# Tiles at multiples of 512 bytes, the last expert batch by token chunk, TensorE's attention groups without a loop, and two output additions in other places

## The reference, cut to what matters

```
x:[64,64,512]
cond[b] = weights[subj[b]]^T x[b] + bias                  # 64x64 per batch element
h   = cond @ WA + bA ; kv, q = halves of h                # each 128 wide
kR  = rope(h @ WB + bB) ; qR = rope(h @ WC + bC)          # 64 wide, q for 16 heads
attn: scores = (q WUQ)(kv WUK)^T + qR kR^T, causal softmax, times (kv WUV), then @ WZ + bZ
x   = x + attn
flat = x @ W^T + adapter(x)                               # low rank, by batch element
logits = flat @ Wg + bg ; top 2 of 4 experts ; each expert takes its top 1024 tokens
y_e = gelu(flat[tokens] @ W1[e]) @ W2[e] * p ;  x[tokens] += y_e
```

## Time and profile before

| | |
|---|---|
| time, median of 3 runs | 1913.26 us (1910.33 to 1914.07) |
| the profiled execution | 1914.91 us, of which the span from the first to the last instruction is 1912.7 us |
| mean granted TensorE clock | 0.985 of full speed |
| busy time | PE 1820.7 us, DVE 925.2 us, ACT 630.4 us, POOL 703.3 us |
| absorb weights | 0 to 47 us of the span |
| attention | 47 to 950 us, 111.3 us for a group |
| routing | 950 to 1163 us |
| experts | 1163 to 1893.3 us, about 90.5 us for a batch |
| after the last matmul | 1893.3 to 1912.7 us |

### The profile page before, as it was taken

One profiled execution on the slowest core, in us unless ns is written; L12 is line 12 of the kernel. 1 busy time (PEld: TensorE's weight loads), 2 busy tenths in 40 slices (PEclk: granted clock), 3 DMA queues, 4 the chain that ended last, 5 costly groups with the idle time before them and its releaser, 6 DMA issues. The chain is left out here.

```text
span 1912.7 us, 29404 instructions
## 1 busy us (share of the span) xinstructions
PE 1820.7 (95%) x10664; PEld 1417.9 (74%) x10664; DVE 925.2 (48%) x1581; ACT 630.4 (33%) x1088; POOL 703.3 (37%) x525
## 2 busy tenths in 40 slices
PE   6799999999999999999999997999999999999996
PEld 4577776767777676777687776888888888888884
DVE  4565667566666656656423783242423333333321
ACT  4333333333333333333223112333333333333331
POOL 1231322123132212313000034565657575757563
PEclk9999999999999999999999998999999999999998
DMA  7000101010010201002132115033304220522001
GB/s 261 23 1 17 52 6 62 7 61 2 17 51 6 62 7 62 1 17 62 37 106 105 61 61 191 19 88 110 66 0 110 99 55 0 132 88 44 9 13 22
DMA packets 68587, 104.80 MB, mean 55 GB/s; under 512 B 12304, under 2 KB 29456, under 8 KB 68496
## 3 DMA queue, kind: packets, MB, share of 16 engines
q1 hardware_dynamic: 53568, 76.92, 12.1%
q0 software_dynamic: 7200, 16.78, 4.8%
q10 hardware_dynamic: 7728, 9.71, 1.4%
HBM read 78.23 MB, written 25.17 MB: 54 GB/s over the span
## 5 line engine op out<-in xcount | busy, mean ns | idle before, releaser
L1858 DVE CAST hh<-hid 128x512 fp32r<-128x512 f32 x128 | 92.5, 723 | 453.1 <-ACT hid L1803 453.1
L1728 POOL TENSOR_TENSOR w1l<-w_raw,w1h 128x512 fp32r<-128x512 f32 x112 | 185.1, 1653 | 153.3 <-ACT w1h L1795 153.2
L441 POOL TENSOR_TENSOR prob<-prob,rinv 128x512 f32<-128x512 f32 x64 | 70.4, 1100 | 465.4 <-DVE rinv L700 465.4
L95 PE MATMUL bank_o<-Mh,mix_h 128*128 128x512 f32 x512 | 211.4, 413 | 20.5 <-DVE x_res L707 19.1
L95 PE MATMUL e_h<-xh,w1h 128*128 (+1 forms) x512 | 203.5, 397 | 5.6 <-POOL w1l L1728 5.6
L96 PE MATMUL e_h<-xl,w1h 128*128 (+1 forms) x512 | 202.6, 396 | 0.0
L97 PE MATMUL e_h<-xh,w1l 128*128 (+1 forms) x512 | 202.5, 395 | 0.0
L97 PE MATMUL bank_o<-Mh,mix_l 128*128 128x512 f32 x512 | 202.1, 395 | 0.0
L96 PE MATMUL bank_o<-Ml,mix_h 128*128 128x512 f32 x512 | 201.7, 394 | 0.0
L95 PE MATMUL e_y<-w2h,hh 128*128 128x512 f32 x512 | 201.2, 393 | 0.0
L96 PE MATMUL e_y<-w2l,hh 128*128 128x512 f32 x512 | 200.6, 392 | 0.0
(11 more groups left out here) (303 smaller groups left out, 3486.9 us busy)
## 6 DMA issues: line engine op xcount, KB each, us to landing
w_raw<-in_W_dram SPq DMA_DIRECT2D x56, 512.0 KB, 4.5
stage<-in_x_dram SPq DMA_DIRECT2D x8, 1024.0 KB, 5.8
x_res<-in_x_dram SPq DMA_DIRECT2D x32, 256.0 KB, 3.5
out_dram<-x_res SPq DMA_DIRECT2D x32, 256.0 KB, 2.0
flat_dram<-flat_sb ACTq DMA_DIRECT2D x32, 256.0 KB, 2.0
rows<-out_dram SPq DMA_DIRECT2D x4, 1024.0 KB, 5.3
stage<-in_W_dram SPq DMA_DIRECT2D x8, 512.0 KB, 5.4
x_res<-out_dram SPq DMA_DIRECT2D x3, 1024.0 KB, 5.1
```

What stands on the lines that cost most here:

```text
L95: nc.tensor.matmul(out, ah, bh, start=start and n == 0, stop=False)
L441: nc.gpsimd.tensor_tensor(prob[:, i % 2, :, :], prob[:, i % 2, :, :], rinv[:, :].unsqueeze(2).to_broadcast([P, HB, C]), ALU.mult).then_inc ...
L1728: nc.gpsimd.tensor_tensor(w1l[:, k, :, :], w1_at(pair, chunk), w1h[:, k, :, :].bitcast(F32), ALU.subtract).then_inc(S["w1_lo"], 1)
L1858: nc.vector.tensor_copy(hh[:, k, :], hid[:, k, :]).then_inc(S["h_hi"], 1)
```

## The change

Allocation: every tile that TensorE reads starts at a multiple of 512 bytes. Small tiles go to the front, to the end of the early region (`SMALL_AT`) or behind the large ones, and `align` fills what is left. Line numbers move by one to some sixty for that. The constant column `part` becomes a table and a transfer of its own.

TensorE's attention program is written out for all 8 groups; the other engines keep the loop. TensorE's program grows from 1881 to 4019 rows.

```diff
@@ absorb_weights, VectorE
-                if i == 1:
+                if i == 2:
                     dve.wait_ge(small_in, SMALL)
...
-                if i in (1, 2):
-                    spread_weights(nc, K, dve, 0, range((i - 1) * GB // 2, i * GB // 2))
+                    spread_weights(nc, K, dve, 0, range(GB))
@@ attention, VectorE
                 queries_rope(g, 6)
+                x2_tile(g, 0)
                 queries_rope(g, 7)
-                x2_tile(g, 0)
...
-                    queries_rope(g + 1, 0)
-                    queries_rope(g + 1, 1)
+                    for u in range(UB - 1):
+                        queries_rope(g + 1, u)
                 x2_tile(g, 5)
                 if more:
-                    queries_rope(g + 1, 2)
-                    queries_rope(g + 1, 3)
+                    queries_rope(g + 1, UB - 1)
@@ attention, TensorE
-            over_groups(pe, first, body)
+            first()
+            for g in range(NG):
+                body(g, g < NG - 1)
@@ experts, GpSimd, last batch
-                    scatter(b, range(CH))
+                    w1_low(END - 2, 0, b, PAIRS - 1, 0)
+                    w2_low(END - 3, 1, b, PAIRS - 2, 1)
+                    w1_low(END - 1, 1, b, PAIRS - 1, 1)
+                    w2_low(END - 2, 2, b, PAIRS - 1, 0)
+                    w2_low(END - 1, 3, b, PAIRS - 1, 1)
+                    pool.wait_ge(S["index_out"], NB)
+                    for c in range(CH):
+                        pool.wait_ge(S["y_ev"], b * CH + c + 1)
+                        pool.indirect_dma_start(out_rows, ..., y_sb[:, c, :], ...)
@@ experts, TensorE, last batch
+            def held(b):
+                hidden(END - 4, 0, b)
+                spend(END - 5, 1)
+                for k in range(1, HELD):
+                    hidden(END - HELD + k, k % 2, b)
+                for c in range(CH):
+                    cols = slice(c * P, (c + 1) * P)
+                    for k in range(HELD):
+                        if c == 0:
+                            pe.wait_ge(S["h_lo"], END - HELD + k + 1)
+                            pe.wait_ge(S["w2_lo"], END - HELD + k + 1)
+                        last = split_product(nc, bank_y[c][:, :], [((hh[:, k, cols], hl[:, k, cols]),
+                                                                    (w2h[:, k, :], w2l[:, k, :]))],
+                                             start=False, stop=k == HELD - 1)
+                    last.then_inc(S["y_mm"], 1)
@@ allocation
+LINE = 512
+def align(nc, ctx, name):
+    short = -(-(-nc.sbuf_base // 32) * 32) % LINE
+    if short:
+        ctx.enter_context(nc.sbuf_tensor(f"pad_{name}", [1, short // 4], F32))
```

More of the change, by code:

```diff
@@ L55 @@
 TABLES = {
-    "always": {"ident": P, "ones": P, "part": 1},
+    "always": {"ident": P, "ones": P},
+    "column": {"part": 1},
     "attend": {"mask": NU // 2 * C, "cosq": NU * C, "sinq": NU * C, "cosk": C, "sink": C},
@@ L1674, in experts @@
         Y0 = 2
+        END = NB * HC
         def over_batches(eng, first, body):
@@ L1693, in rounds @@
             after_two()
-            with eng.Fori(1, LOOP) as i:
+            with eng.Fori(1, LOOP if more else LOOP - 1) as i:
                 two(i)
-            last = b * HC + HC
-            one(last - 2, 0, (b + 1, 0, 0) if more else None, (b, PAIRS - 1, 1))
-            one(last - 1, 1, (b + 1, 0, 1) if more else None, (b + 1, 0, 0) if more else None)
+            if more:
+                last = b * HC + HC
+                one(last - 2, 0, (b + 1, 0, 0), (b, PAIRS - 1, 1))
+                one(last - 1, 1, (b + 1, 0, 1), (b + 1, 0, 0))
         def out_free(eng, b):
@@ L1834, in first @@
                 one(1, 1, (0, 1, 1), (0, 1, 0))
+            def held(b):
+                gelu(END - 4, 0, 0)
+                w1_high(END - 2, 0, b, PAIRS - 1, 0)
+                act.wait_ge(S["y_mm"], END - 4 + Y0)
+                w2_high(END - 3, 1, b, PAIRS - 2, 1)
+                gelu(END - 3, 1, 1)
+                w1_high(END - 1, 1, b, PAIRS - 1, 1)
+                w2_high(END - 2, 2, b, PAIRS - 1, 0)
+                gelu(END - 2, 0, 2)
+                w2_high(END - 1, 3, b, PAIRS - 1, 1)
+                gelu(END - 1, 1, 3)
+                out_free(act, b)
+                for c in range(CH):
+                    act.wait_ge(S["y_mm"], END - HELD + Y0 + c + 1)
+                    nc.scalar.activation(y_sb[:, c, :], bank_y[c][:, :], ACT.Copy,
+                                         scale=R["gate"][:, bass.ds(b * CH + c, 1)]).then_inc(S["y_ev"], 1)
             def body(b, more):
-                for i in range(LOOP):
+                for i in range(LOOP if more else LOOP - 1):
                     for k in range(2):
                         one(b * HC + 2 * i + 2 + k, k, (b, i + 2, k), (b, i + 1 + k, 1 - k))
+                if not more:
+                    held(b)
+                    return
                 last = b * HC + HC
[L1841 to L1849, removed]
+                x_high(b + 1)
+                one(last - 2, 0, (b + 1, 0, 0), (b, PAIRS - 1, 1))
+                one(last - 1, 1, (b + 1, 0, 1), (b + 1, 0, 0))
+                one(last, 0, (b + 1, 1, 0), (b + 1, 0, 1), between=lambda: gated(b))
+                one(last + 1, 1, (b + 1, 1, 1), (b + 1, 1, 0))
             over_batches(act, first, body)
@@ L1885, in body @@
                     index_in(b + 1)
-                with dve.Fori(0, LOOP) as i:
+                with dve.Fori(0, LOOP if more else LOOP - 1) as i:
                     for k in range(2):
@@ L1892, in body @@
                 nc.vector.tensor_copy(tok_out[:, :], R["token"][:, bass.ds(b * CH, CH)]).then_inc(S["index_out"], 1)
-                if more:
-                    x_low(b + 1)
+                if not more:
+                    for k in range(HELD):
+                        one(END - HELD + k, k)
+                    return
+                x_low(b + 1)
                 one(last - 2, 0)
                 one(last - 1, 1)
-                if more:
-                    one(last, 0)
+                one(last, 0)
                 gated(b)
-                if more:
-                    one(last + 1, 1)
+                one(last + 1, 1)
             over_batches(dve, first, body)
@@ L1942, in body @@
                 n = b * HC
-                with pe.Fori(0, LOOP) as i:
+                with pe.Fori(0, LOOP if more else LOOP - 1) as i:
                     for k in range(2):
@@ L1960, in body @@
                 spend(last - 2, 0)
-                if more:
-                    pe.wait_ge(S["xt_lo"], b * TC + TC)
-                    hidden(last, 0, b + 1)
+                pe.wait_ge(S["xt_lo"], b * TC + TC)
+                hidden(last, 0, b + 1)
                 spend(last - 1, 1, stop=True)
[L1965 to L1968, removed]
+                hidden(last + 1, 1, b + 1)
+                pe.wait_ge(S["y_ev"], (b + 1) * CH)
+                spend(last, 0, start=True)
             over_batches(pe, first, body)
@@ L1989, in block_program @@
         K.parts = {}
+        load_table(nc, ctx, K, "column")
+        for name, shape in (("wg", [P, TC, NE]), ("bias", [P, 5])):
+            K[name] = ctx.enter_context(nc.sbuf_tensor(name, shape, F32))
+        K.update(bA=K["bias"][:, 0:2], bB=K["bias"][:, 2:3], colsum=K["bias"][:, 3:5])
+        K["subj"] = ctx.enter_context(nc.sbuf_tensor("subj", [NSUB, B], I32))
+        align(nc, ctx, "front")
         load_table(nc, ctx, K, "always")
```

76 lines of the change are left out of this document (45 added, 31 removed).

## The result

The changed kernel takes 1902.77 us (median of 5 runs, 1901.03 to 1903.53), the kernel before in the same runs 1911.48 us (1910.33 to 1914.07): the ratio is 0.994, 95% interval 0.9927 to 0.9954. It became faster by 8.7 us, where 31 us were forecast. The direction is right and the time lies in the range, but the size is less than a third.

The account below looks back on a forecast made before the run. The prediction took TensorE, working in 95% of the span, as the bound. Its terms, -21 - 10 - 8 + 15 - 6.5 - 0.5 = -31 us, gave 1882 us at the median, with a range of 1862 to 1908.

Parts of the forecast that it names:

- x2_tile(g, 5) behind a rotation: Attention's seventh output projection: DVE adds one rotation later, TensorE idles 2.10 us more in seven groups; +15 us.
- The upper bound of +23: For x2_tile(g, 5): the moved addition also runs slower beside POOL's multiplications, 7 x 1.13 = 8 us more.
- Alignment: 512-column matmuls: equal tile starts by 512 bring all rows to the fast 226.8 ns spacing; -21 us.
- x2_tile(g, 0): Attention's second output projection: adding ahead of query 7's rotation removes 0.97 us TensorE idling in eight groups; -8 us.
- the last batch: Last expert batch: banks come 12 matmuls apart, so three of four scatters have gone when the last comes; -6.5 us.
- The prediction's account of 256 as harmless: Matmul tile starts: spacing stays slow, 232 to 233 ns, where remainders by 512 differ by other than 256.
- Rival A: Alignment does nothing on TensorE: sum -10 us, time 1903 us; chance 0.20.
- Groups without a loop: TensorE's attention groups written out: the stall at six loop tops reached by a jump goes; -10 us.
- The start: Start: DVE's copies of the subjects' matrices come a step later, TensorE's 3.3 us wait for low parts goes; -0.5 us.
- Rival B: The addition behind the third rotation costs nothing, as DVE gets there earlier: 1867 us; chance 0.10.
- rival C: With all tiles at whole lines, matmul spacing falls below the fast rows too: 1845 us at half, 1808 all; chance 0.08.
- Rival D: TensorE's longer program outruns its instruction fetch, 1.4 us a stall: 1937 us, with fewer stalls about 1920; chance 0.07.

Follow-up runs that it names:

- the kernel with the addition put back: Changed kernel with x2_tile(g, 5) put back behind the rotation of query 1: 1867.74 us, ratio to the kernel before 0.975.
- The kernel with three pairs set apart: Against the kernel with the addition put back: mix 64 bytes against M, w1h and w1l 256 against xh, hh and hl 128 against w2; 1887.69 us, ratio 0.9862.

## Why the prediction was wrong

The step that failed is "x2_tile(g, 5) behind a rotation". Its mechanism was named rightly: TensorE already waits there, the addition comes 2.1 us later, and TensorE does not get the time back. The wait grew by 2.4 us. But the term was put at +15 us and measures +35: the prediction counted only the idle time, at the clock as it was. A wait of 4.0 us also takes the clock to 0.50, and TensorE loses 2.6 us more in each of seven groups after the wait is over. The upper bound of +23 came from another mechanism and missed this too. Useless work in the wait gave 17 us back with the addition as late as before, so this part is shown and not only argued.

The trace of before had the sign of it, in the stretch of the wait for `Al` whose 3.3 us the prediction used. Its windows:

```profile
34.00:37.00 3.00, 0.53 (x2) 0.00 (x0) 2.88 (x5) 0.88 (x2) 1.73 (x1) 0.99 1.05 384
37.00:40.00 3.00, 2.18 (x9) 2.21 (x10) 3.00 (x6) 0.10 (x1) 0.00 (x0) 0.50 0.34 124
40.00:43.00 3.00, 3.00 (x4) 1.01 (x3) 2.10 (x7) 1.07 (x2) 0.00 (x0) 0.50 0.01 3
43.00:46.00 3.00, 3.00 (x14) 1.77 (x12) 1.43 (x3) 1.83 (x4) 0.00 (x0) 0.87 0.00 0
```

TensorE is idle most of the first stretch, and the clock is at 0.50 in the next two. The waits of 1.5 us for this addition, of which the kernel before has seven, leave it at full. The length of a wait does not decide alone, though: of the six gaps at the loop's top one, of 1.58 us, is followed by a slow stretch as well, which the prediction also passed over. The timeline's row behind this gap, and the windows of the stretch (columns as above):

```profile
646.50 0.65 PE L884 MATMUL bank_s<-k_absorbed,q 128*64 128x256 f32 x3 [1.58 <-issue]
...
644.00:647.00 3.00, 1.42 (x10) 0.53 (x8) 0.42 (x1) 0.59 (x1) 0.00 (x0) 1.00 0.47 126
647.00:650.00 3.00, 3.00 (x43) 2.05 (x43) 2.01 (x3) 0.37 (x1) 0.00 (x0) 0.65 0.70 188
```

So the question to ask of a wait that grows from 1.5 to 3.6 us was which of these it will resemble. The Trainium skill says under "TensorE: Matmul & The Clock Gate", section "HAM oscillation — how this bites in real kernels", that idle gaps in TensorE's stream cost clock beyond their own length; the runs agree, with 2.6 us beside 2.4.

The other steps, each with what the runs show:

- **Alignment**, -21 us: right, with its size in part estimated. By the spacings in the rows, 2.80 to 2.72 and 2.74 to 2.72 us for twelve and 232.3 to 227.7 ns, the three kinds of matmul give 10 + 3 + 7 = 20 us, an estimate. No run undoes this edit alone: what the loop (12 to 16 us), `x2_tile(g, 0)` and the last batch leave of the 47.5 us by which the kernel with the addition put back is faster is 16 to 22. The experts' matmuls took 9.6 us less, where 12 were forecast. The kernel with three pairs set apart is 20 us slower, but it sets other pairs apart than the kernel before, the fast one on `e_y` among them; it shows that the starts alone can cost this much. That the relation of the starts matters and not the multiple of 512 was the reading of the prediction, and the shift by 32 bytes shows it. The gain on `e_y`, whose tiles had equal starts already, does not follow from that reading: it comes with the hidden matmuls in front of them, as above. The prediction's account of 256 as harmless holds in the later steps of a row of matmuls. Rival A is out. The Trainium skill's rule on TensorE's two independent read ports ("SBUF — State Buffer", section "Who interferes with whom") leaves no room for an effect of the starts; the runs, with 233 against 227 ns, show one.
- **Groups without a loop**, -10 us: right in attention's span, 11.8 us and within its bounds of -8 and -13; in the medians it is 16, outside them.
- **x2_tile(g, 0)**, -8 us: right, 8 to 9 us.
- **The last batch**, -6.5 us: right, 5.6 to 6.5 us.
- **The start**, -0.5 us: nothing measurable, within its bounds.

With +35 in place of +15 the prediction's sum is -11 us, against -8.7 measured. Rival B (no cost) is out by the 35 us, and rival C did not occur: hidden matmuls average 226.7 ns, where the earlier trace rows have 226.8. Rival D's gaps do not show in the written-out groups.

## What to carry to other kernels

A wait of the bounding engine is not worth its length alone: look at the granted clock behind the longest waits in the trace, and price a wait that grows as idle time plus the slow stretch that may follow. When a step is moved past another on a busy engine, ask in both directions what each of its parts frees: here the best place for an addition was between a rotation's shuffle, which frees a buffer for someone else, and the rest of the rotation, for which no new wait of TensorE appeared. And when operands of equal matmuls run at two speeds, compare the starts of their tiles before looking for waits.

## What the runs showed of the hardware that was not expected

- TensorE's clock fell to 0.50 in a wait of 3.9 to 4.0 us or within 1.5 us behind it, in 7 groups of 7 in both kernels that had it. It stayed at full in every wait of 1.3 to 1.7 us for the same addition, but fell behind one of six gaps of 1.1 to 1.7 us at the loop's top of the kernel before, so the length of a gap does not decide alone. Filling 2.7 of the 4.0 us with matmuls whose result is never read made the kernel 17 us faster.
- The distance, by 512, of the starts of the moving tile and the stationary tile changes the spacing of 512-column matmuls: 227 ns at 0, 233 at 64 and 128. At 256 it is 226.7 in the last steps of twelve, and some 4 ns more in the first seven, behind wider-spaced matmuls; matmuls whose own tiles have equal starts are slowed there in the same way. A shift of all tiles by 32 bytes changes nothing.
